# Graph attention kernel: in the spread stage one compare scalar per tile and three sums per edge lane instead of one

## The chip, the cores and the metric

The kernel runs on one core of a Trainium2 chip. The time is device microseconds of one execution; three runs of the kernel before gave 6165.33, 6170.83 and 6172.71 us. The core has five engines with queues of their own: PE (matrix products), DVE (vector work), ACT (activation functions, copies), POOL (GpSimd, here also the issuer of scattered writes) and SP (issues DMAs). They meet through semaphores only.

## The reference

A graph of 6250 nodes with 64 features and 206,250 edges (source, destination, 64 edge features), sorted by destination. First a graph attention layer with four heads, then two graph convolutions, each followed by a layer norm.

```python
out_i = act(jnp.concatenate([x_i, edge_attr], -1) @ W).reshape(-1, HEADS, DIM)   # act = softplus
out_j = act(jnp.concatenate([x_j, edge_attr], -1) @ W).reshape(-1, HEADS, DIM)
alpha = act((jnp.concatenate([out_i, out_j], -1) * att).sum(-1))
...                                    # norm over all edges, softplus, softmax over the edges of i
msg = out_j * alpha[:, :, None]
aggr = jax.ops.segment_sum(msg, i, num_segments=N_NODES)
...
msgs = h[src] * norm[:, None]          # graph convolution, twice
out = jax.ops.segment_sum(msgs, dst, num_segments=n)
```

## The kernel before, in words

`i` of the attention layer is the source, `j` the destination. Edges come sorted by destination, but the attention layer sums over sources. So the kernel puts them in another order in DRAM, and the stages follow one another, with a barrier between.

**Key stage** (`key_stage`). From the lists of sources and destinations it makes the counts and, for every edge, a pair of numbers in DRAM: minus the source's lane (its number modulo 128) and a code. The code is the source's block (number / 128) times 8, plus the destination modulo 8, plus 1024 times the destination's bin, which is the destination / 8. It also finds where each of the 784 bins begins in the sorted list (`startS`), and sets a flag when the data do not suit the fast path (then other, general stages run).

**Spread stage** (`spread_stage`, lines 710 to 1180). 202 steps of 1024 edges, 128 partitions by K = 8. In each step:
- PE, ACT: the destination's half of the layer, `out_j`, 256 numbers an edge (`product` L1120, `softplus` L1033, written into the tile `rowS`).
- DVE: `rank` (L927) finds the row of each edge in the new order. `dots` (L973) multiplies the 64 numbers of one head with their attention weights and sums them, for head 0 alone (DOTS = 1), in two parts of four lanes each.
- POOL: eight scattered writes a step (L889), each of 128 rows of RW = 323 numbers: 256 of `out_j`, 64 edge features, minus the source's lane, the destination, and the sum of head 0. A part is sent when its sums are made.
- In the first 196 steps, four bins a step: the counts matrix of the graph (`adj`), which the convolutions use. For each bin `load_pairs` (L835) on SP's queue fetches the pairs of the 384 edges that begin at the bin's start. `column` (L955) on DVE makes for each of three groups of 128 edges two one-hot tiles: `one_c` (L962), 392 columns of blocks by destination modulo 8, and `one_s` (L964), 128 lanes. L962 adds the bin's own number from `codes` to the column's number and compares the sum with the pair's code, so edges that belong to a later bin fall out. PE multiplies the two (L1144), ACT copies the counts (L1030), and after four steps, a block of 128 destinations, ACT stores 1568 KB (L1070).

What sets the order: each engine's queue is written out by hand. DVE's step is: rank, with two of the three columns of bin 1 put between its dependent instructions; the third column; bin 2; the one-hots of the next step's ranks and window (`hots`, `windows`); bin 3; part 0 of the sums; bin 0 of the next step; part 1 of the sums. On SP's queue, in the first 100 steps, two fills of 323 KB follow each block. Four `rowS` buffers let POOL be up to that many steps behind.

**Half stage** (`half_stage`). It reads the rows back in the new order, 912 tiles of 256 rows, in groups of BU = 6 with a buffer each. A buffer is loaded again (L1592) when the sums of its tile are made (`sp_read`). DVE makes one of the tile's two one-hots three tiles ahead (`places`, L1624), POOL the other (L1604), and POOL copies the edge features (L1612) and the lanes and ready sums (L1606). PE transposes them (`turn`), one tile ahead of the products (`product`, L1721 and L1726); its queue is in order, so the products of a tile wait for the transposes of the next. Then ACT (L1682, L1686), then DVE (`finish`, L1627): for each of 2 × 4 heads one sum. For head 0 only the source's half is still to sum, 64 numbers (L1638), and the ready part is added later (L1659); for heads 1 to 3 both halves, 128 numbers (L1643).

Later stages read the first 256 numbers of the rows; the softmax, message, node and convolution stages are not touched.

Of the kernel before, what the change touches and what calls it, by code (L numbers as in the profile page):

```python
# [15 lines left out]
fp32 = mybir.dt.float32  # L16
# [6 lines left out]
P = 128  # L23
# [15 lines left out]
DOTS = 1  # L39
DOT = C + D + 2  # L40
RW = DOT + DOTS
NR_BUF = 4
GQ = GB // NR_BUF
CODE = 1024
EXACT = 256
# [8 lines left out]
class Sizes:  # L54


    def __init__(self, nodes, edges):
# [20 lines left out]
        assert self.GC < CODE and self.GC <= 1024  # L78
# [80 lines left out]
def gnn_kernel(nc, x, src, dst, ea, W, att, bias, gamma, beta, W1, b1, W2, b2, out):  # L159
# [11 lines left out]
    def sb(ctx, name, shape, dt, side=None):  # L171
        return ctx.enter_context(nc.sbuf_tensor(own(name), shape, dt, side=side))
# [16 lines left out]
    with top:  # L189
# [33 lines left out]
        with ExitStack() as lists:  # L223
            m["ioc"] = sb(lists, "ioc", [P, z.GC], fp16)
# [45 lines left out]
def key_stage(nc, z, m, sb, ps, sem, x, src, dst):  # L270

    NB, HB, NG, T = z.NB, z.HB, z.NG, z.NG * K
    with ExitStack() as ctx:
# [12 lines left out]
        flatl = sb(ctx, "flatl", [P, T], i32)  # L286
# [30 lines left out]
        none = sb(ctx, "none", [P, GT, 2], fp32)  # L317
        psq = [ps(ctx, f"psq{n}", [P, 512], fp32) for n in range(2)]
# [90 lines left out]
        def _(eng):  # L409
# [14 lines left out]
            eng.iota(m["ioc"][:, :], [[1, z.GC]], base=0, channel_multiplier=0,  # L424
# [7 lines left out]
            eng.memset(blank[:, :, C + D:C + D + 1], 1.0).then_inc(blanked, 1)  # L432
# [15 lines left out]
        def _(eng):  # L448
# [21 lines left out]
            eng.tensor_scalar(flatl[:, :], flat[:, 0:T], EXACT - 1, None, ALU.bitwise_and).then_inc(v, c.up() and 1)  # L470
            eng.tensor_scalar(eighth[:, :], flat[:, 0:T], 3, None, ALU.arith_shift_right).then_inc(v, c.up() and 1)
            eng.wait_ge(v, c.n)
            eng.tensor_copy(flatb[:, :], flatl[:, :]).then_inc(low_ready, 1)
# [23 lines left out]
            eng.wait_ge(loaded, 16 * loads)  # L497
            eng.tensor_scalar(tmp[:, :, :], key[:, :, :], 7, None, ALU.arith_shift_right).then_inc(v, c.up() and 1)
# [11 lines left out]
            for n in range(2):  # L510
# [3 lines left out]
            eng.scalar_tensor_tensor(m["ends"][:, :, 0], tmp[:, 0, :], -1.0, neg[:, 0, :], ALU.mult,  # L514
                                     ALU.subtract).then_inc(v, c.up() and 1)
            eng.tensor_copy(m["ends"][:, :, 1].bitcast(i32), m["dst"][:, :]).then_inc(v, c.up() and 1)
# [7 lines left out]
            eng.scalar_tensor_tensor(neg[:, 1, :], tmp[:, 0, :], float(CODE), tmp[:, 1, :], ALU.mult,  # L524
                                     ALU.add).then_inc(v, c.up() and 1)
# [30 lines left out]
            eng.tensor_tensor(m["bad"][0:1, :], m["bad"][0:1, :], full8[:, :], ALU.add).then_inc(v, c.up() and 1)  # L556

# [152 lines left out]
def spread_stage(nc, z, m, sb, ps, sem, ea, att):  # L710
# [4 lines left out]
    with ExitStack() as ctx:  # L715
# [191 lines left out]
        def _(eng):  # L907
# [47 lines left out]
            def column(b, s, q, k):  # L955
                t = step(b, s)
                r = q % 2
                if k == 0:
                    eng.wait_ge(pair_in[q], (t + 1) * 16)
                    o, c = before(t, q, 2, GQ)  # L960
                    wait(eng, built[o], c)
                eng.tensor_scalar(one_c[r][:, k, :], m["ioc"][:, :], m["codes"][:, span(t * GQ + q, 1)],  # L962
                                  pair[q][:, k, 1:2], ALU.add, ALU.is_equal)
                ins = eng.tensor_scalar(one_s[r][:, k, :], m["io128b"][:, :], pair[q][:, k, 0:1], 0.0, ALU.add,  # L964
                                        ALU.is_equal)
                if k == GT - 1:
                    ins.then_inc(cols_made[q], 1)

            def adj(b, s, q):
                for k in range(GT):  # L970
                    column(b, s, q, k)
# [435 lines left out]
def table_stage(nc, z, m, sb, ps, sem, W):  # L1407
# [5 lines left out]
    with ExitStack() as ctx:  # L1413
# [47 lines left out]
        def _(eng):  # L1461
# [3 lines left out]
            eng.memset(fill[:, :, C + D:C + D + 1], 1.0).then_inc(zeroed, 1)  # L1465
# [1611 lines left out]
```

## Time and profile before

| | us |
|---|---|
| timed runs, median (lowest, highest) | 6170.83 (6165.33, 6172.71) |
| profiled execution, span | 6164.4 |
| DVE busy in the span | 4909.2 (80%) |
| PE busy | 4650.4 (75%) |
| ACT busy | 3996.8 (65%) |
| POOL busy | 3765.3 (61%) |
| spread stage, DVE / POOL busy in 290 to 2455 us | 1880 / 1648 |

The profile is of one execution, which the profiler times by its span. A row of a stretch gives each engine's busy time in it; a row of waits says who stood idle until what came; a row of the order of time gives start and duration in us, and in brackets the idle time before it and what ended that. Durations of neighbours on one engine overlap a little, so the distance from start to start is what an instruction costs. Issuing, register and semaphore instructions do not count as busy.

### The profile page before, as it was taken

To read this page: it belongs to the slowest core of one execution; us is meant where nothing else is said; L and a number is where in the kernel's file an instruction comes from. 1 tells how busy PE (TensorE), PEld (TensorE's weight loads), DVE (VectorE), ACT (ScalarE), POOL (GpSimd) and SP (SyncE) were. 2 spreads that over 40 slices of the span, in tenths; PEclk is the share of its full clock that TensorE was granted. 3 is DMA by queue.
4 is the path that set the end of the run, shared out by engine and by line. 5 is a ranking of instruction groups with operands and counts; after the bars stand their busy time and mean duration, and the time that the engine had idled before them with its cause. 6 is when DMAs were issued, how large, how long until landed. Compare 5 with 4: busy or idle time off the path is not lost. (4 is left out here: it accounts for less than half of the span.)

```text
span 6164.4 us, 164058 instructions
## 1 busy us (share of the span) xinstructions
PE 4650.4 (75%) x32887; PEld 3049.3 (49%) x32888; DVE 4909.2 (80%) x27493; ACT 3996.8 (65%) x10575; POOL 3765.3 (61%) x5381
## 2 busy tenths in 40 slices
PE   1377777777777774788888888888658888885799
PEld 0144444444444443445544544444335555554799
DVE  6588888989988984799999999999867777667233
ACT  3266666667666664688888888888767777776000
POOL 2277777777777777566666656565457777775000
PEclk8599999999999997899999999999879999997899
DMA  8867777776666665655555555555447777774898
GB/s 215 243 219 237 233 228 237 225 237 225 218 221 225 216 221 176 197 156 157 156 157 156 159 155 155 155 155 154 112 138 217 219 218 217 216 216 134 315 360 339
DMA packets 913878, 1262.07 MB, mean 205 GB/s; under 512 B 268468, under 2 KB 775459, under 8 KB 894916
## 3 DMA queue, kind: packets, MB, share of 16 engines
q1 hardware_dynamic: 785592, 859.76, 48.3%
q0 software_dynamic: 88560, 318.29, 14.0%
q10 hardware_dynamic: 39580, 82.35, 3.8%
q8 instruction: 57, 0.93, 0.1%
q14 instruction: 89, 0.73, 0.0%
HBM read 833.17 MB, written 426.91 MB: 204 GB/s over the span
## 5 line engine op out<-in xcount | busy, mean ns | idle before, releaser
L889 POOL DMA_INDIRECT rows<-rowS,idx x1616 | 1647.8, 1020 | 530.6 <-issue 505.7
L1643 DVE CUSTOM_DVE_ANT_1 junk<-bufh,attb 128x128 bf16<-128x128 f32 x5472 | 1369.1, 297 | 0.0
L1604 POOL TENSOR_SCALAR one<-io128b,bufh 128x128 bf16<-128x128 bf16 x912 | 752.8, 825 | 802.6 <-DMA bufh<-rows 802.6
L962 DVE TENSOR_SCALAR one_c<-ioc,codes,pairS 128x392 bf16<-128x392 f16 x2352 | 916.3, 390 | 214.3 <-DMA pairS<-pairs 205.5
L2369 PE MATMUL psm<-msg,onem 128*128 128x260 f32 x3648 | 916.1, 395 | 208.6 <-issue 168.9
L1144 PE MATMUL psa<-one_c,one_s 128*128 128x392 bf16 x2352 | 550.2, 345 | 546.2 <-ACT cnts L1030 297.7
L2290 POOL TENSOR_TENSOR msg<-oj,heads 128x512 f32<-128x512 f32 x760 | 799.8, 1075 | 209.7 <-DMA oj<-rows 176.9
L2369 PEld LDWEIGHTS psm<-msg,onem 128*128 128x128 f32 x3648 | 649.5, 190 | 474.8 <-issue 399.4
L1726 PE MATMUL pre<-P3h,oneT 128*128 x5472 | 756.4, 274 | 0.0
L1682 ACT ACTIVATE lg<-pre 128x512 f32<-128x512 f32 x912 | 545.0, 598 | 297.4 <-PE pre L1726 272.8
L2302 ACT ACTIVATE dist_m<-io,sums_lanes 128x128 f32<-128x128 f32 x1368 | 499.2, 396 | 293.4 <-PE psm L2369 262.6
L964 DVE TENSOR_SCALAR one_s<-io128b,pairS 128x128 bf16<-128x128 bf16 x2352 | 651.4, 277 | 0.0
L1037 ACT ACTIVATE lgS<-preS 128x1024 f32<-128x1024 f32 x404 | 413.2, 1023 | 359.1 <-PE preS L1133 355.1
L1721 PE MATMUL pre<-W2d,eaTh 64*128 64x256 f32 x3648 | 641.7, 429 | 0.0
L1726 PEld LDWEIGHTS pre<-P3h,oneT 128*128 128x128 bf16 x5472 | 460.5, 98 | 344.9 <-issue 302.8
L1686 ACT ACTIVATE bufh<-lg 128x512 f32<-128x512 f32 x912 | 576.5, 632 | 29.0
L1144 PEld LDWEIGHTS psa<-one_c,one_s 128*128 128x128 bf16 x2352 | 195.5, 100 | 720.9 <-DVE one_s L964 519.4
L1030 ACT ACTIVATE cnts<-psa 128x392 bf16<-128x392 f32 x784 | 363.3, 489 | 259.6 <-PE psa L1144 253.7
L1127 PE MATMUL preS<-W2d,eaT 64*128 64x256 f32 x3232 | 514.1, 441 | 6.6 <-ACT eaT L1048 6.6
L1638 DVE CUSTOM_DVE_ANT_0 junk<-bufh,attb 128x64 bf16<-128x64 f32 x1824 | 423.9, 232 | 74.0 <-ACT bufh L1686 70.1
L1710 PE MATMUL turned<-identb,one 128*128 128x128 bf16 x1824 | 255.0, 221 | 300.1 <-DVE one L1624 133.2
L2344 DVE TENSOR_TENSOR acc<-acc,psm 128x260 f32 x912 | 381.6, 418 | 113.2 <-DVE acc L2344 74.6
(299 smaller groups left out, 9020.0 us busy)
## 6 DMA issues: line engine op xcount, KB each, us to landing
bufh<-rows SPq DMA_DIRECT2D x912, 323.0 KB, 3.2
oj<-rows SPq DMA_DIRECT2D x912, 256.0 KB
adj<-adj SPq DMA_DIRECT2D x70, 1568.0 KB, 10.0
adj<-cnts ACTq DMA_DIRECT2D x49, 1568.0 KB
eaS<-in_edge_attr_dram SPq DMA_DIRECT2D x201, 256.0 KB
low<-dlow SPq DMA_DIRECT2D x202, 252.0 KB
adj_early<-adj SPq DMA_DIRECT2D x28, 1568.0 KB, 8.9
rows<-blanktail POOLq DMA_DIRECT2D x20, 1615.0 KB, 43.5
```

The source lines that it names most:

```text
L889: eng.indirect_dma_start(out=m["rows"][h], out_offset=bass.IndirectOffsetOnAxis(ap=idx[s][:, k:k + 1], axis=0), in_=rows[s][:, k, :], in_o ...
L962: eng.tensor_scalar(one_c[r][:, k, :], m["ioc"][:, :], m["codes"][:, span(t * GQ + q, 1)], pair[q][:, k, 1:2], ALU.add, ALU.is_equal)
L964: ins = eng.tensor_scalar(one_s[r][:, k, :], m["io128b"][:, :], pair[q][:, k, 0:1], 0.0, ALU.add, ALU.is_equal)
L1144: mm = eng.matmul(psa[r][:, 0:z.GC], one_s[r][:, k, :], one_c[r][:, k, :], start=(k == 0), stop=(k == GT - 1))
L1604: eng.tensor_scalar(one[j % PRE][:, 1, :], m["io128b"][:, :], buf[j][:, 1, 0, C + D:C + D + 1], 0.0, ALU.add, ALU.is_equal).then_inc(secon ...
L1643: ins = eng.tensor_tensor_reduce(junk[q][:, k * H + h, :, :], buf[j][:, k, :, h * D:(h + 1) * D], attb[:, :, h, :], 1.0, 0.0, ALU.mult, AL ...
L1682: eng.activation(lg[q][:, :, :], pre[q][:, :, 0:C], ACT.Exp, accum_out=m["exps"][:, span(2 * z.NG + i * BU + j, 1)]).then_inc(exp_done[j], 1)
L1686: eng.activation(buf[j][:, :, 1, 0:C], lg[q][:, :, :], ACT.Ln, bias=1.0).then_inc(sp_ready[j], 1)
L1721: eng.matmul(pre[j % PRE][:, k, 0:C], eaT[q][k * D:(k + 1) * D, :], m["W2d"][k * D:(k + 1) * D, :], start=True, stop=False, skip_group_che ...
L1726: mm = eng.matmul(pre[j % PRE][:, k, 0:C], oneT[q][:, k * P:(k + 1) * P], P3[:, bass.ds(b, 1), n, :].rearrange("p o c -> p (o c)"), start= ...
L2290: eng.tensor_tensor(msg[j][:, :, 0:C].rearrange("p k (h d) -> p k h d", h=H), oj[j][:, :, :, :], heads[:, :, j * UT:(j + 1) * UT].rearrang ...
L2369: mm = eng.matmul(psm[j][:, 0:C + H], one[q][:, k, :], msg[q][:, k, :], start=(k == 0), stop=(k == UT - 1))
```

## The change

The code of a pair now holds the destination's bin modulo four, times 512, instead of the bin times 1024. The table of column numbers `ioc` has four rows, one for each bin of a step, with 0, 512, 1024 and 1536 added. So L962's addition of `codes` goes, and the compare has one scalar from memory, the pair's code. `one_s` is compared with the lane itself, no longer with a sum against zero. The order of a bin's six compares is now three `one_c`, then three `one_s`, and the rank has the three `one_c` of bin 1 in its first gap and the three `one_s` in its second. Since a bin is told only modulo four, the key stage tests that bins four apart start at least 384 edges apart, and adds to the flag where they do not.

DOTS is 3: the spread stage sums heads 0, 1 and 2, and the half stage sums only the source's half for these, and both halves for head 3. The row has 325 numbers; destination and lane change places, so that lane and sums lie together.

```diff
-DOTS = 1
+DOTS = 3
 DOT = C + D + 2
+LANE = C + D + 1
...
+TURN = 512
...
-            m["ioc"] = sb(lists, "ioc", [P, z.GC], fp16)
+            m["ioc"] = sb(lists, "ioc", [P, GQ, z.GC], fp16)
...
-            eng.iota(m["ioc"][:, :], [[1, z.GC]], base=0, channel_multiplier=0,
+            eng.iota(m["ioc"][:, :, :], [[TURN, GQ], [1, z.GC]], base=0, channel_multiplier=0,
...
-            eng.tensor_copy(pair[:, :, 0], m["ends"][:, :, 0]).then_inc(v, c.up() and 1)
-            eng.tensor_scalar(tmp[:, 0, :], key[:, 1, :], 3, None, ALU.arith_shift_right).then_inc(v, c.up() and 1)
+            eng.tensor_scalar(pair[:, :, 0], m["ends"][:, :, 1], -1.0, None, ALU.mult).then_inc(v, c.up() and 1)
+            eng.tensor_scalar(tmp[:, 0, :], key[:, 1, :], (GQ - 1) * GD, None, ALU.bitwise_and).then_inc(v, c.up() and 1)
...
+            far = z.NR - GQ
+            eng.tensor_scalar(ended[:, 0:far], startf[:, GQ:z.NR], float(z.E), float(GT * P), ALU.is_ge,
+                              ALU.mult).then_inc(v, c.up() and 1)
+            eng.tensor_tensor(near8[:, 0:far], startf[:, GQ:z.NR], startf[:, 0:far],
+                              ALU.subtract).then_inc(v, c.up() and 1)
+            eng.wait_ge(v, c.n)
+            eng.tensor_tensor(near8[:, 0:far], near8[:, 0:far], ended[:, 0:far], ALU.add).then_inc(v, c.up() and 1)
+            eng.wait_ge(v, c.n)
+            eng.tensor_reduce(close8[:, :], near8[:, 0:far], AX.X, ALU.min).then_inc(v, c.up() and 1)
+            eng.wait_ge(v, c.n)
+            eng.tensor_scalar(close8[:, :], close8[:, :], float(GT * P), None, ALU.is_lt).then_inc(v, c.up() and 1)
+            eng.wait_ge(v, c.n)
+            eng.tensor_tensor(m["bad"][0:1, :], m["bad"][0:1, :], close8[:, :], ALU.add).then_inc(v, c.up() and 1)
...
-            def column(b, s, q, k):
+            def columns(b, s, q):
+
                 t = step(b, s)
                 r = q % 2
-                if k == 0:
-                    eng.wait_ge(pair_in[q], (t + 1) * 16)
-                    o, c = before(t, q, 2, GQ)
-                    wait(eng, built[o], c)
-                eng.tensor_scalar(one_c[r][:, k, :], m["ioc"][:, :], m["codes"][:, span(t * GQ + q, 1)],
-                                  pair[q][:, k, 1:2], ALU.add, ALU.is_equal)
-                ins = eng.tensor_scalar(one_s[r][:, k, :], m["io128b"][:, :], pair[q][:, k, 0:1], 0.0, ALU.add,
-                                        ALU.is_equal)
-                if k == GT - 1:
-                    ins.then_inc(cols_made[q], 1)
+                eng.wait_ge(pair_in[q], (t + 1) * 16)
+                o, c = before(t, q, 2, GQ)
+                wait(eng, built[o], c)
+                for k in range(GT):
+                    eng.tensor_scalar(one_c[r][:, k, :], m["ioc"][:, q, :], pair[q][:, k, 1:2], None, ALU.is_equal)
+
+            def lanes(b, s, q):
+
+                r = q % 2
+                for k in range(GT):
+                    ins = eng.tensor_scalar(one_s[r][:, k, :], m["io128b"][:, :], pair[q][:, k, 0:1], None,
+                                            ALU.is_equal)
+                ins.then_inc(cols_made[q], 1)
...
                 def between(k):
                     if dense(b):
-                        column(b, s, 1, k)
+                        (columns, lanes)[k](b, s, 1)
 
                 rank(b, s, h, between)
                 if dense(b):
-                    column(b, s, 1, 2)
                     adj(b, s, 2)
...
                     eng.tensor_copy(m["sums"][:, 0:1 + DOTS, span((i * BU + j) * UT, UT)],
-                                    buf[j][:, :, 0, C + D:DOT + 1:2].rearrange("p k n -> p n k"))\
+                                    buf[j][:, :, 0, LANE:DOT + DOTS].rearrange("p k n -> p n k"))\
```

On DVE, at the start of a step of the spread stage, the order before was this (`ranks` and `base` belong to the rank, `one_c` and `one_s` to a bin):

```order
L942 TENSOR_TENSOR ranks<-psr,base 128x400
L962 TENSOR_SCALAR one_c<-ioc,codes,pairS 128x392
L964 TENSOR_SCALAR one_s<-io128b,pairS 128x128
L948 TENSOR_TENSOR base<-base,psr 128x50
L950 TENSOR_TENSOR ranks<-ranks,ohr 128x400
L962 TENSOR_SCALAR one_c<-ioc,codes,pairS 128x392
L964 TENSOR_SCALAR one_s<-io128b,pairS 128x128
L953 TENSOR_REDUCE idx<-ranks 128x8
L962 TENSOR_SCALAR one_c<-ioc,codes,pairS 128x392
L964 TENSOR_SCALAR one_s<-io128b,pairS 128x128
```

In the changed kernel the same place reads:

```order
L960 TENSOR_TENSOR ranks<-psr,base 128x400
L981 TENSOR_SCALAR one_c<-ioc,pairS 128x392 x3
L966 TENSOR_TENSOR base<-base,psr 128x50
L968 TENSOR_TENSOR ranks<-ranks,ohr 128x400
L987 TENSOR_SCALAR one_s<-io128b,pairS 128x128 x3
L971 TENSOR_REDUCE idx<-ranks 128x8
L981 TENSOR_SCALAR one_c<-ioc,pairS 128x392 x3
L987 TENSOR_SCALAR one_s<-io128b,pairS 128x128 x3
```

Bin 1 is now finished before the reduction that makes `idx`, and each group of three compares of one kind stands together. After bin 3, and again after bin 0 of the next step, 12 sums follow where there were 4.

In the half stage DVE's sums for one of a tile's two columns of rows were these (the row with 128x1 reads the sum out of the accumulator):

```order
L1638 ISA junk,sums<-bufh,attb 128x64
L1638 ISA sums 128x1
L1643 ISA junk,sums<-bufh,attb 128x128
L1643 ISA sums 128x1
L1643 ISA junk,sums<-bufh,attb 128x128
L1643 ISA sums 128x1
L1643 ISA junk,sums<-bufh,attb 128x128
L1643 ISA sums 128x1
```

And in the changed kernel:

```order
L1659 ISA junk,sums<-bufh,attb 128x64
L1659 ISA sums 128x1
L1659 ISA junk,sums<-bufh,attb 128x64
L1659 ISA sums 128x1
L1659 ISA junk,sums<-bufh,attb 128x64
L1659 ISA sums 128x1
L1664 ISA junk,sums<-bufh,attb 128x128
L1664 ISA sums 128x1
```

The number of instructions is the same; two of the four sums are of half the length.

## Rows read from the trace of the kernel before

**Rows 1.** The page, its first line.

```profile
span 6164.4 us, 164058 instructions
```

**Rows 2.** Busy us (and count) by stretch, then PE clock, DMA share, GB/s.

```profile
core 0: us, PE busy (x) PEld busy (x) DVE busy (x) ACT busy (x) POOL busy (x), PEclk, DMA share, GB/s
...
290.00:2455.00 2165.00, 1564.62 (x12214) 980.32 (x12214) 1880.23 (x9397) 1404.25 (x2398) 1647.78 (x1616) 0.93 0.69 223
...
2600.00:4200.00 1600.00, 1377.92 (x9796) 797.63 (x9796) 1493.80 (x13070) 1322.87 (x3770) 965.45 (x2261) 1.00 0.56 156
```

**Rows 3.** Half stage, 2600 to 4200 us: loads of row tiles, and one wait.

```profile
bufh<-rows SPq DMA_DIRECT2D x754, 323.0 KB, 3.2
...
DVE junk L1638 <- ACT bufh L1686: 55.5, 111, 0.9
```

**Rows 4.** Waits, 290 to 2455 us: total us, times, longest.

```profile
POOL rows L889 <- issue: 505.7, 1570, 24.8
...
DVE one_c L962 <- DMA pairS<-pairs: 205.5, 49, 7.2
```

**Rows 5.** Order of time, DVE, spread stage: start, duration, engine, line.

```profile
1012.79 0.23 DVE L940 COPY rowS<-ends 128x16 f32 x1
...
1022.29 0.23 DVE L940 COPY rowS<-ends 128x16 f32 x1
...
1027.30 0.48 DVE L924 TENSOR_SCALAR ohT<-low,wsc 126x1024 bf16<-126x1024 bf16 x1
1027.69 0.37 DVE L962 TENSOR_SCALAR one_c<-ioc,codes,pairS 128x392 bf16<-128x392 f16 x1
1027.99 0.24 DVE L964 TENSOR_SCALAR one_s<-io128b,pairS 128x128 bf16<-128x128 bf16 x1
1028.15 0.37 DVE L962 TENSOR_SCALAR one_c<-ioc,codes,pairS 128x392 bf16<-128x392 f16 x1
...
1029.34 0.22 DVE L979 CUSTOM_DVE_ANT_0 weighed<-rowS,att_row 128x64 bf16<-128x64 f32 x1
1029.49 0.22 DVE L979 CUSTOM_DVE_ANT_0 weighed<-rowS,att_row 128x64 bf16<-128x64 f32 x1
1034.58 0.38 DVE L962 TENSOR_SCALAR one_c<-ioc,codes,pairS 128x392 bf16<-128x392 f16 x1 [4.86 <-DMA pairS<-pairs]
```

**Rows 6.** Order of time: the spread stage's last sum and last scatter.

```profile
2419.94 0.22 DVE L979 CUSTOM_DVE_ANT_0 weighed<-rowS,att_row 128x64 bf16<-128x64 f32 x1
...
2452.61 0.96 POOL L889 DMA_INDIRECT rows<-rowS,idx  x1 [0.30 <-issue]
```

**Rows 7.** Order of time, half stage: one loop from sums to sums.

```profile
3097.53 0.28 DVE L1643 CUSTOM_DVE_ANT_1 junk<-bufh,attb 128x128 bf16<-128x128 f32 x1
3097.74 0.27 DVE L1624 TENSOR_SCALAR one<-io128b,bufh 128x128 bf16<-128x128 bf16 x1
...
3101.51 0.76 POOL L1604 TENSOR_SCALAR one<-io128b,bufh 128x128 bf16<-128x128 bf16 x1 [1.19 <-DMA bufh<-rows]
...
3103.09 0.70 PE L1721 MATMUL pre<-W2d,eaTh 64*128 64x256 f32 x4
...
3106.07 0.29 DVE L1638 CUSTOM_DVE_ANT_0 junk<-bufh,attb 128x64 bf16<-128x64 f32 x1 [0.46 <-ACT bufh L1686]
```

**Rows 8.** One line each: durations and starts, or mean ns after the bar.

```profile
L962 DVE TENSOR_SCALAR one_c<-ioc,codes,pairS x2352: 362/373/586, 290.3 to 2360.8; 128x392 bf16<-128x392 f16 x196
...
L889 POOL DMA_INDIRECT rows<-rowS,idx x1616 | 1647.8, 1020 | 530.6 <-issue 505.7
...
L889 POOL DMA_INDIRECT rows<-rowS,idx x1616: 956/962/1431, 300.0 to 2452.6; - x180
...
L559 DVE TENSOR_SCALAR_CACHE_REDUCE hit<-hi_src 128x800 bf16<-128x800 bf16 x50 | 49.3, 986 | 1.7
```

**Rows 9.** Order of time: issues on SP's and ACT's queues.

```profile
1022.28 1.55 SPq L1403 DMA_DIRECT2D rows<-fill  x2
...
1022.71 0.34 ACTq L1070 DMA_DIRECT2D adj<-cnts  x1
```

More of the change, by code:

```diff
@@ L77, in __init__ @@
         self.NR = self.NB * GB
-        assert self.GC < CODE and self.GC <= 1024
+        assert self.GC + GD <= TURN and GQ * TURN <= 2048
 class Count:
@@ L317, in key_stage @@
         none = sb(ctx, "none", [P, GT, 2], fp32)
+        near8, ended = (step[0:1, :] for step in steps8)
+        close8 = sb(ctx, "close8", [1, 1], fp32)
         psq = [ps(ctx, f"psq{n}", [P, 512], fp32) for n in range(2)]
@@ L469, in _ @@
             eng.wait_ge(flat_in, 64)
-            eng.tensor_scalar(flatl[:, :], flat[:, 0:T], EXACT - 1, None, ALU.bitwise_and).then_inc(v, c.up() and 1)
+            eng.tensor_scalar(flatl, flat[:, 0:T], EXACT - 1, None, ALU.bitwise_and).then_inc(v, c.up() and 1)
             eng.tensor_scalar(eighth[:, :], flat[:, 0:T], 3, None, ALU.arith_shift_right).then_inc(v, c.up() and 1)
             eng.wait_ge(v, c.n)
-            eng.tensor_copy(flatb[:, :], flatl[:, :]).then_inc(low_ready, 1)
+            eng.tensor_copy(flatb[:, :], flatl).then_inc(low_ready, 1)
             eng.tensor_copy(base8[:, :], eighth[:, 0:1]).then_inc(v, c.up() and 1)
@@ L523, in _ @@
             eng.wait_ge(v, c.n)
-            eng.scalar_tensor_tensor(neg[:, 1, :], tmp[:, 0, :], float(CODE), tmp[:, 1, :], ALU.mult,
-                                     ALU.add).then_inc(v, c.up() and 1)
+            eng.scalar_tensor_tensor(neg[:, 1, :], tmp[:, 0, :], float(TURN // GD), tmp[:, 1, :],
+                                     ALU.mult, ALU.add).then_inc(v, c.up() and 1)
             eng.wait_ge(v, c.n)
@@ L953, in rank @@
                     eng.tensor_reduce(idx[s][:, :], ranks[:, :, :], AX.X, ALU.add).then_inc(idx_ready, 1)
-            def column(b, s, q, k):
+            def columns(b, s, q):
                 t = step(b, s)
                 r = q % 2
-                if k == 0:
-                    eng.wait_ge(pair_in[q], (t + 1) * 16)
-                    o, c = before(t, q, 2, GQ)
-                    wait(eng, built[o], c)
-                eng.tensor_scalar(one_c[r][:, k, :], m["ioc"][:, :], m["codes"][:, span(t * GQ + q, 1)],
-                                  pair[q][:, k, 1:2], ALU.add, ALU.is_equal)
-                ins = eng.tensor_scalar(one_s[r][:, k, :], m["io128b"][:, :], pair[q][:, k, 0:1], 0.0, ALU.add,
-                                        ALU.is_equal)
-                if k == GT - 1:
-                    ins.then_inc(cols_made[q], 1)
+                eng.wait_ge(pair_in[q], (t + 1) * 16)
[9 more added lines that the diff above has]
+                ins.then_inc(cols_made[q], 1)
             def adj(b, s, q):
-                for k in range(GT):
-                    column(b, s, q, k)
+                columns(b, s, q)
+                lanes(b, s, q)
             def dots(b, s, part):
@@ L1623, in places @@
                 wait(eng, o_turned[o], c)
-                eng.tensor_scalar(one[q][:, 0, :], m["io128b"][:, :], buf[j][:, 0, 0, C + D:C + D + 1], 0.0,
+                eng.tensor_scalar(one[q][:, 0, :], m["io128b"][:, :], buf[j][:, 0, 0, LANE:LANE + 1], 0.0,
                                   ALU.add, ALU.is_equal).then_inc(one_ready[j], 1)
@@ L1842, in places @@
                 wait(eng, o_turned[o], c)
-                eng.tensor_scalar(one[q][:, 0, :], m["io128b"][:, :], buf[j][:, 0, 2 * D:2 * D + 1], 0.0,
+                eng.tensor_scalar(one[q][:, 0, :], m["io128b"][:, :], buf[j][:, 0, 2 * D + 1:2 * D + 2], 0.0,
                                   ALU.add, ALU.is_equal).then_inc(one_ready[j], 1)
-                eng.tensor_copy(m["nloA"][:, span((i * BU + j) * UT, UT)], buf[j][:, :, 2 * D]).then_inc(lo_kept[j], 1)
+                eng.tensor_copy(m["nloA"][:, span((i * BU + j) * UT, UT)], buf[j][:, :, 2 * D + 1]).then_inc(lo_kept[j], 1)
             def finish(i, j):
```

17 lines of the change are left out of this document (9 added, 8 removed).

## The prediction

> **What bounds the kernel now.** I read the page first, then the busy time by stretch, then in each of the two touched stages the waits, and last the order of time inside one period of each.
>
> The span is 6164.4 us [rows 1]; the three timed runs have a median of 6170.8, so some 6 us lie around the span, and my sum is made on the span and given with those 6 added. Two stages carry the change. The spread stage runs from 290 to 2455 us, the half stage from about 2494 to about 4430: there 754 rows tiles are loaded in 1600 us [rows 2, 3], 2.12 us a tile, and it has 912 tiles.
>
> In the spread stage DVE is busy 1880 of 2165 us and POOL 1648 [rows 2], yet POOL is the bound. The reader is to see three things. POOL's idle time is 505.7 us in 1570 pieces put down to "issue" [rows 4], 0.3 us between one scatter and the next, so with a scatter of 0.96 us its least period is 1.26 us and 8 scatters a step cost at least 10.1 us. DVE, in a step without a wait, needs 9.50 us (from one copy of the ends at 1012.79 to the next at 1022.29 [rows 5]). And at the end DVE makes its last sum at 2419.94 and POOL starts its last scatter at 2452.61 [rows 6]: POOL is three steps behind. But DVE is nearly as full: it also waits 205.5 us for the pair lists, 49 times [rows 4], once for each of the 49 blocks. 196 × 9.5 + 205 = 2067 us against POOL's 2036 plus what collisions add. So DVE has no cover to give away: what DVE is given here beyond some 30 us is on the path.
>
> In the half stage DVE is busy 1494 of 1600 us and PE 1378 [rows 2], and TensorE's granted clock is 1.00, its upper level of 2.4 GHz. DVE looks like the bound, with 8 sums a tile. But it is not alone. Follow one loop [rows 7]. DVE ends the sums of a tile at 3097.74 (there the next tile's one-hot starts), which frees the tile's buffer; the next rows land and POOL starts its one-hot on them at 3101.51, 3.77 us later; POOL also copies the edge features, and only then does PE transpose them and start the product of the tile before, at 3103.09, 1.58 us later; PE, two ACT passes, and DVE starts the sums of that tile at 3106.07, 2.98 us later, having waited 0.46 us for ACT. These 8.33 us contain no sum at all. They span five tiles, and DVE waits at their end once in each group of six (111 waits, 55.5 us in the stretch [rows 3]).
>
> **What the change does, and what it costs.**
>
> Spread stage, sums. 202 steps × 8 lanes × 2 more heads = 3232 more sums on DVE. Two of them start 0.15 us apart (1029.34 and 1029.49, with the accumulator read between [rows 5]). 16 × 0.15 = 2.40 us a step; in the 196 steps that have bins, 470 us. Nothing hides them: DVE goes from one instruction to the next without a gap.
>
> Spread stage, one scalar in place of two in one_c. The trace has no fp16 tile compared with one scalar. The one_s instruction (128 elements, one scalar from memory) takes 0.16 us to the next start, ohT (1024 elements, one scalar) 0.39, one_c (392, two scalars) 0.30 [rows 5]. A line through the first two is 0.127 + 0.257 ns an element, so 392 elements with one scalar would take 0.23: 0.06 to 0.07 less than now. Taken: 0.065 × 2352 [rows 8] = 153 us. Below, it can be 0 (the second scalar is free and one_c is slow for its type); above, one_c cannot be cheaper than one_s with a third of its elements, so at most 0.14 × 2352 = 329. The row it is nearest to is the line's. one_s keeps one scalar in memory and loses only a constant: 0.
>
> The Trainium skill (VectorE: DVE Perf Modes, the section on the TRN2 errata) gives SBUF work on DVE as 58 cycles plus the elements over the mode's speed, with no term for the scalars. That rule speaks against this change: it would have one_c cost the same with one scalar as with two, and the 153 us would be 0. The rows do not bear it out, since one_c lies 0.07 us over the line of its neighbours; but they do not separate the second scalar from the other type, so it stays a rival, below.
>
> Spread stage, the wait for pairs. At the start of a block the queue of SP has two fills of 323 KB (first half only) at 1022.28 and ACT's store of 1568 KB goes out at 1022.71 [rows 9]; DVE comes for its pair list at 1029.6 and gets it at 1034.58, 4.86 us late [rows 5]: about 12 us from the store to the landing. With the longer step DVE comes later after that store: 1.6 us by the rest of the step in which the store goes out, 0.6 by its own next step up to that point, and perhaps 1 because the three compares of a tile now stand together ahead of the reduction, so that PE, ACT and the store get on sooner. Some 3 us of a mean wait of 4.2 go: 49 × 3 = 150 us. Bounds: 0 and 205.
>
> The end of the stage. The last compare starts at 2360.8 [rows 8]. 2361 + 470 − 153 − 150 = 2528. Then follow six steps without bins, in which POOL is the bound with 10.1 us each, 61 us, and about 5 us for its last part: 2594 against 2453.6. The stage grows by 140 us; POOL, now ahead of DVE, waits. With the bounds of the wait it is 85 to 290, with those of the scalar −35 to 295.
>
> POOL's scatters average 1020 ns and half of them take 962 or less [rows 8]; the rest is collisions with DVE. The Trainium skill (SBUF — State Buffer, "Who interferes with whom") says that DVE's two-port modes lock GpSimd out for the whole instruction. Shorter compares would by that cost POOL less than the 94 us they may cost now, but POOL no longer ends last, so the sum is the same.
>
> Half stage. Heads two and three come summed, so 4 of 8 sums a tile go from the 128-element form, 0.21 us (3097.53 to 3097.74 [rows 7]), to the 64-element form, 0.15: 0.26 us a tile at most counting 0.065 each. If DVE alone bound, 912 × 0.26 = 237 us. But the loop above has no sum in its 8.33 us. A group of six is now the first tile 1.88, the loop 8.33, the sums of the last tile 1.80 and 0.7 for the copies and the loop's branch, together 12.7, which is 6 × 2.12. After: 1.62 + 8.33 + 1.54 + 0.7 = 12.2. The four tiles in the middle save their 0.26 too, but wait for it at the loop's end. 152 groups × 0.52 = 79 us. Bounds: 237 above; below 40, if the denser loads lengthen the 3.77 us.
>
> The rest. The copies of sums (POOL's now 4 rows, DVE's addition now 3 heads) move one cost to another: 0. Rows are 1300 bytes, not 1292: 0.6% more bytes where the DMA share is 0.69 and 0.56 [rows 2]. The key stage gets six short instructions on one partition, of at most 784 elements; a row of 800 takes 0.99 us [rows 8]: +4 us. The longer iota is hidden by DVE's wait for the inputs.
>
> Sum: 6170.8 + 140 + 4 − 79 = 6236 us.
>
> **Rivals.**
>
> A, faster: the half stage gives all of its 237 us. It would if POOL's part of the loop shrinks as well, since POOL reads while DVE sums, or if buffers land sooner; then 6170.8 + 144 − 237 = 6078. It decides from about 0.16 us saved per tile on. For it: DVE is busy 93% there. Against it: the wait for ACT, once a group, is there already now. A milder form with the waits for pairs all gone and 150 us from the half stage gives 6110. Together 20%.
>
> B, no change: the same two in part, half stage 130 to 160 us: 6160 to 6180. 9%.
>
> C, the second scalar is free (the errata rule above): 153 us more, 6389; at half that price, 6310. 10%.
>
> D, the wait for pairs stays at 205 us since the store ends it and the store moves along with the step: 150 more, 6386. For it: the store follows the step's last tile. 10%.
>
> E, POOL stays the bound and hides the new sums: the stage stays at 2165 and the kernel takes about 6095. It needs a DVE step under 10.6 us; 9.50 + 2.40 − 0.78 = 11.1 before any wait. 3%, counted in A.
>
> F: the added test on near starts sets the flag and the general path runs, at least a second half stage, over 8000 us. Four bins hold about 1000 edges and the test asks for 384: 1%.
>
> **The numbers.** My forecast, 6236, has about 50%; its own range is 6190 to 6290. Taking in part of A below and of C and D above, 8 in 10 lie in 6120 to 6330. A change of under 0.2%, 12 us, can't be told from none. Faster by more: 20%; within: 9%; slower: 71%.
>
> **What would show it.** In the spread stage: one_c about 320 ns at the median in place of 373, dots 24 a step, a step of 11.1 us, POOL with real waits for DVE's sums, ACT's waits for sent rows gone, waits for pairs near 60 us. In the half stage: a tile of 2.03 us, DVE busy under 90%, and its wait for ACT grown to some 200 us or more. The forecast is wrong if a half-stage tile takes under 1.95 us, if one_c's duration does not fall, or if POOL is still never idle in the spread stage.

## The result, and the profile after

The changed kernel takes 6537.9 us (median of 4 runs, 6537.3 to 6545.8), the one before, on the same chip, 6168.7 (6165.3 to 6172.7): a ratio of 1.0594, 95% interval 1.0579 to 1.0609. The forecast was 6236, the range 6120 to 6330. The profiled execution's span grew from 6164.4 [rows 1] to 6544.1 us, by 380.

First the page after, of which three lines matter: the span and two of the DMA queues (packets, MB, share of 16 engines' time). The instruction queue q14 had 89 packets and 0.73 MB before.

```profile
span 6544.1 us, 169809 instructions
...
q14 instruction: 313, 2.56, 0.1%
q8 instruction: 57, 0.93, 0.1%
```

Then the stretches of the two stages, which answer to [rows 2]. The columns are the same.

```profile
290.00:2925.00 2635.00, 1697.20 (x12220) 1045.51 (x12218) 2189.03 (x15861) 1418.62 (x2399) 1589.66 (x1616) 0.84 0.56 184
3100.00:4700.00 1600.00, 1437.55 (x10309) 848.31 (x10309) 1397.08 (x13744) 1373.92 (x3968) 939.48 (x2380) 1.00 0.60 165
```

The spread stage is 470 us longer (2635 against 2165), and DVE is busy in it for only 309 us more. DVE was busy 87% of the stage before, 83% after: it has more to do and stands idle more. The half stage runs denser, as forecast. So the question is what DVE's new idle time is. These are the waits of the spread stage after (total us, times, longest), to be read against [rows 4]:

```profile
POOL rows L907 <- issue: 484.9, 1417, 26.6
POOL rows L907 <- DVE rowS L1001: 374.7, 71, 11.9
DVE rowS L958 <- issue: 341.6, 43, 10.9
...
DVE ohr L932 <- issue: 42.2, 22, 2.8
...
DVE one_c L981 <- DMA pairS<-pairs: 14.3, 6, 4.4
```

The wait for pairs went from 205.5 us to 14.3. In its place DVE stands 341.6 us ahead of L958 and 42.2 us ahead of L932, and "issue" says that nothing which the profile shows held it. POOL, which before waited 3.0 us for DVE's sums in all, now waits 374.7. The order of time on DVE shows where this lies, in a block of the first half of the destinations:

```profile
1209.62 0.21 DVE L1001 CUSTOM_DVE_ANT_0 weighed<-rowS,att_row 128x64 bf16<-128x64 f32 x1
...
1209.76 0.21 DVE L1001 CUSTOM_DVE_ANT_0 weighed<-rowS,att_row 128x64 bf16<-128x64 f32 x1
1209.90 0.08 DVE L1001 DVE_READ_ACCUMULATOR2_ANT rowS<- 128x1 f32 x1
1215.89 0.18 DVE L958 COPY rowS<-ends 128x16 f32 x1 [5.91 <-issue]
...
1218.76 0.78 DVE L981 TENSOR_SCALAR one_c<-ioc,pairS 128x392 bf16<-128x392 f16 x3
1219.45 0.57 DVE L987 TENSOR_SCALAR one_s<-io128b,pairS 128x128 bf16<-128x128 bf16 x3
1221.78 0.58 DVE L932 TENSOR_TENSOR ohr<-io,hi_src 128x400 bf16<-128x400 bf16 x1 [1.77 <-issue]
```

and in one of the second half:

```profile
2541.80 0.18 DVE L958 COPY rowS<-ends 128x16 f32 x1 [10.87 <-issue]
...
2545.85 0.57 DVE L932 TENSOR_TENSOR ohr<-io,hi_src 128x400 bf16<-128x400 bf16 x1
```

L958 is the first instruction of DVE's loop body, which holds one block of four steps. There are two such loops, one for each half of the destinations, of 23 and 22 passes; the first and the last block of a half stand outside as straight code. In the first loop there is a gap of some 6 us at the start of a pass and one of some 1.9 us a little later; in the second one of about 10 us and no second one. The 43 gaps ahead of L958 are 22 and 21: one each time that a loop returns to its start, none at its first pass.

### The profile page after: what moved, and what is told of

It reads as the page before. It is cut to its first block and busy times, and to the rows that moved or that the text cites. A ratio compares the mean times of both kernels' runs of the same rounds, so it can differ in the third digit from the quotient of the medians.

```text
span 6544.1 us, 169809 instructions
## 1 busy us (share of the span) xinstructions
PE 4771.8 (73%) x32887; PEld 3123.7 (48%) x32888; DVE 5020.0 (77%) x33963; ACT 3990.7 (61%) x10575; POOL 3621.3 (55%) x5381
## 5 line engine op out<-in xcount | busy, mean ns | idle before, releaser
L907 POOL DMA_INDIRECT rows<-rowS,idx x1616 | 1589.7, 984 | 1056.4 <-issue 484.9
L1165 PE MATMUL psa<-one_c,one_s 128*128 128x392 bf16 x2352 | 571.1, 357 | 889.2 <-DVE one_s L987 837.3
L1625 POOL TENSOR_SCALAR one<-io128b,bufh 128x128 bf16<-128x128 bf16 x912 | 715.7, 785 | 796.0 <-DMA bufh<-rows 795.7
L1659 DVE CUSTOM_DVE_ANT_0 junk<-bufh,attb 128x64 bf16<-128x64 f32 x5472 | 1018.0, 233 | 146.2 <-ACT bufh L1707 129.7
L1001 DVE CUSTOM_DVE_ANT_0 weighed<-rowS,att_row 128x64 bf16<-128x64 f32 x4848 | 743.2, 216 | 3.1 <-ACT rowS L1061 3.1
L981 DVE TENSOR_SCALAR one_c<-ioc,pairS 128x392 bf16<-128x392 f16 x2352 | 627.3, 319 | 23.4 <-DMA pairS<-pairs 14.3
L1148 PE MATMUL preS<-W2d,eaT 64*128 64x256 f32 x3232 | 571.4, 482 | 7.0 <-ACT eaT L1069 7.0
L1664 DVE CUSTOM_DVE_ANT_1 junk<-bufh,attb 128x128 bf16<-128x128 f32 x1824 | 534.7, 293 | 0.0
L987 DVE TENSOR_SCALAR one_s<-io128b,pairS 128x128 bf16<-128x128 bf16 x2352 | 457.7, 251 | 0.0
```

The costliest lines, as they stand in the source:

```text
L907: eng.indirect_dma_start(out=m["rows"][h], out_offset=bass.IndirectOffsetOnAxis(ap=idx[s][:, k:k + 1], axis=0), in_=rows[s][:, k, :], in_o ...
L981: eng.tensor_scalar(one_c[r][:, k, :], m["ioc"][:, q, :], pair[q][:, k, 1:2], None, ALU.is_equal)
L1001: ins = eng.tensor_tensor_reduce(weighed[:, k, n, :], rows[s][:, k, n * D:(n + 1) * D], att_row[:, n, :], 1.0, 0.0, ALU.mult, ALU.add, row ...
L1148: eng.matmul(pre[h][:, q, a * C:(a + 1) * C], eaT[j][q * D:(q + 1) * D, 2 * h + a, :], m["W2d"][q * D:(q + 1) * D, :], start=(a == 0), sto ...
L1165: mm = eng.matmul(psa[r][:, 0:z.GC], one_s[r][:, k, :], one_c[r][:, k, :], start=(k == 0), stop=(k == GT - 1))
L1625: eng.tensor_scalar(one[j % PRE][:, 1, :], m["io128b"][:, :], buf[j][:, 1, 0, LANE:LANE + 1], 0.0, ALU.add, ALU.is_equal).then_inc(second_ ...
```

## The experiments

Theory A, a guess that the experiments were to test: DVE's instruction memory holds four pieces of 128 instructions and loads one piece ahead of the one it is in. A loop that touches at most three pieces stays in it. One that touches four pushes out its own start, and each pass begins with a load of instructions from DRAM. I counted every instruction of DVE's list (waits, register operations and branches too). The loop body of the spread stage had 260 and has 372. The trace's records agree: 260 and 372 a pass, and in the changed kernel 1049 from the first loop's last return to the second's first. (The list has one jump to the very next instruction in between that the trace does not record, and it is not counted.) Where a piece begins was fitted to one observation: the small gap of the first half stands ahead of the loop's 27th instruction (L932), so the loop's first is at place 102 of a piece (counted from 0). Every other place follows by counting. B is the same with two pages of 256, C that the place of the code does not matter.

All ten kernels were timed in three rounds against the kernel before on their chips (there 6189 to 6194 us, 0.3 to 0.4% more than on the chip of the result, so that times of different rows are best compared by their ratios). "Last sum" is the start of the last L1001 of the spread stage, "half" the time from the half stage's first sum to its last, both in the profiled execution. Pieces are those that DVE's two loops of the spread stage touch. "Once" and "in 2" are single gaps outside the loops, behind the inserted increments; 1.6 us of the gaps of experiments 1 and 5 and the 0.7 and 0.6 us of 6 and 7 are of that kind too.

| kernel | pieces | gaps ahead of the loop, us | wait for pairs | last sum | half | ratio (95%) |
|---|---|---|---|---|---|---|
| before | 3, 3 | 0 | 205.5 | 2419.9 | 1931 | 1 |
| changed | 4, 4 | 341.6 + 42.2 | 14.3 | 2888.6 | 1835 | 1.0594 (1.0579 to 1.0609) |
| 1 changed, shifted 30 | 3, 4 | 121.9 | 88.3 | 2704.0 | 1839 | 1.0252 (1.0235 to 1.0269) |
| 2 changed, both loops shifted | 3, 3 | 10.7 in 2 | 98.2 | 2593.6 | 1842 | 1.0091 (1.0074 to 1.0108) |
| 3 codes only | 3, 3 | none | 266.8 | 2374.7 | 1937 | 0.9898 (0.9881 to 0.9914) |
| 4 two heads | 3, 4 | 196.5 | 99.5 | 2565.1 | 1888 | 1.0128 (1.0111 to 1.0145) |
| 5 before, shifted 32 | 4, 3 | 191.1 | 97.9 | 2535.2 | 1939 | 1.0147 (1.0130 to 1.0164) |
| 6 two heads, shifted | 3, 3 | 0.7 | 135.6 | 2411.8 | 1889 | 0.9877 (0.9861 to 0.9894) |
| 7 as 6, pairs early | 3, 3 | 0.6 | 1.8 | 2376.6 | 1891 | 0.9823 (0.9806 to 0.9840) |
| 8 as 3, pairs early | 3, 3 | none | 2.4 | 2363.3 | 1936 | 0.9871 (0.9855 to 0.9888) |
| 9 before, shifted 64 | 3, 3 | 4.5, once | 218.9 | 2439.5 | 1936 | 0.9996 (0.9987 to 1.0006) |
| 10 as 2, pairs early | 3, 3 | 10.7 in 2 | 2.0 | 2496.3 | 1839 | 0.9933 (0.9916 to 0.9949) |

**1. The changed kernel, shifted.** Thirty increments of a semaphore that nobody waits for, ahead of DVE's first loop:

```diff
+        padded = sem(ctx, "padded")
             eng.wait_ge(att_row_in, 16)
+            for _ in range(30):
+                eng.sem_inc(padded, 1)
             by_half(eng, blocks)
```

> The changed kernel with 30 semaphore increments more on DVE's queue ahead of its first loop of the spread stage; nothing else differs, and they cost about 1 us. Three theories of the gaps at the start of DVE's loop (341.6 us before L958, 42.2 us before L932 in the changed kernel). Theory A: the loop's 372 instructions are fetched again on each pass because they touch four pieces of 128 instructions (a piece is one 8 KB packet of the instruction queue), and only a loop that touches three stays. The 30 instructions move the first loop (destinations of the first half) onto three pieces, the second loop stays on four: the gaps of about 6 + 1.6 us a pass go in the first loop (some 170 us), those of 10.4 us stay in the second; as the waits for pairS come back in part (about 2 us a block, 50 us), the time is about 6400 us. Theory B: the same with two pages of 256 instructions: both loops then fit, no gap is left, 6200 to 6250 us. Theory C: the gap has nothing to do with where the code lies (a full DMA queue, a late semaphore at the start of a block): nothing changes, 6538 us.

It took 6351.6 us against 6192.9. The waits of DVE, first in 290 to 1450 us, then in 1450 to 2740:

```profile
DVE one_c L982 <- DMA pairS<-pairs: 84.3, 25, 6.5
...
DVE rowS L959 <- issue: 1.6, 1, 1.6
```

```profile
DVE rowS L959 <- issue: 120.4, 21, 6.9
...
DVE one_c L982 <- DMA pairS<-pairs: 4.0, 3, 3.1
```

The first loop lost its gaps, the second kept one at each return: A and neither B nor C. The instruction queue says the same more directly. From 450 to 1300 us, inside the first loop, the queue moves no packet at all; from 1600 to 2600 us, some 20 passes of the second, it moves

```profile
q14 instruction: 101, 0.83, 0.3%
```

which is five a pass: the four pieces of the loop and one ahead. In the changed kernel the first of these stretches has 81 packets, in the kernel before none. The second loop now begins at place 29, so that 99 of its instructions lie in the first piece, and its gap fell from 10 to 5.7 us, which I had not expected (I had left it at 10.4, hence 6400 for the time). This fits the two patterns of the changed kernel: where few instructions stand ahead of the next piece (1 in the second half, 26 in the first), the pass seems to wait for that piece too. No run tests this reading by itself.

**2. Both loops shifted.** 30 increments ahead of the first loop and 104 between the two, so that they begin at places 4 and 5.

> The changed kernel with 30 semaphore increments ahead of DVE's first loop of the spread stage and 104 more between its two loops (some 5 us). Theory A (pieces of 128 instructions): both loops of 372 instructions now touch three pieces; all gaps go, 384 us less, and about 50 to 100 us of waits for pairS come back: 6210 to 6280 us, where the prediction (6236 us) had put the change itself. The instruction queue's packets fall from 313 to about 90. Theory B: with two pages of 256 the first loop fits and the second too: as A. Theory C (address doesn't matter): 6538 us plus 5.

6248.9 us, inside what was expected, with 98 packets on q14, and neither loop has a gap. DVE's waits from 290 to 2630 us:

```profile
DVE one_c L982 <- DMA pairS<-pairs: 98.2, 42, 6.1
DVE rowS L959 <- issue: 10.7, 2, 9.1
```

The two gaps left (1.6 us at 293.6 and 9.1 at 1483.2) stand in straight code right behind the 30 and the 104 increments, which take about 0.1 us each and do not count as busy: they are the price of the shift. 134 instructions without any work, on the engine that sets the stage, take the ratio from 1.0594 to 1.0091. This is the change as the prediction had priced it, 0.9% slower.

```profile
290.00:2630.00 2340.00, 1653.93 (x12218) 1022.06 (x12216) 2192.47 (x15861) 1419.21 (x2398) 1611.33 (x1616) 0.90 0.65 207
```

DVE is busy 2192 us as in the changed kernel (2189), in 295 us less of time.

**3 and 4. The codes alone (DOTS = 1), and two heads (DOTS = 2)**, each a change of one line: `DOTS = 3`.

> The changed kernel with DOTS = 1: the codes modulo four with one scalar, but only head 0 is summed in the spread stage, as before. The loop has 244 instructions and touches three pieces: no gaps. Half stage as before. If DVE's step sets the block: 2352 one_c less by 0.065 us each, 153 us, so 6020 us if the waits for pairS do not grow. Rival: each block ends no sooner because the loads of pairS (205.5 us of waits before) are held by what lies ahead of them on SP's queue, so that the waits grow by what one_c loses: 6150 to 6170 us. Taken value 6090 us.

> The changed kernel with DOTS = 2: heads 0 and 1 summed in the spread stage. DVE's loop has 308 instructions; by its place the first loop touches three pieces of 128, the second four. Theory A: no gaps in the first loop, gaps of about 10 us a pass in the second (22 passes, 220 us). Sum from before: +1616 sums of 0.15 = +242, one_c -153, gaps +220, waits for pairS -110 (they go in the second loop), half stage -48: about 6320 us. Theory B (two pages of 256): the second loop, from place 127 or 255 of a page, is cut as well only if a page begins right behind its start: the same. Theory C (gaps come with DVE's work in a step or with the queue's load): about equal gaps in both loops or none in either.

The codes alone: 6127.6 us, 1% faster than before, where 6090 was taken, between 6020 and a rival of 6150 to 6170: neither holds whole. DVE's busy time fell by 138 us (1880 to 1742), the wait for pairs rose from 205.5 to 266.8, and the last sum came only 45 us earlier. POOL's row of the whole stage shows why (busy, mean ns of one, then idle time):

```profile
L907 POOL DMA_INDIRECT rows<-rowS,idx x1616 | 1606.1, 994 | 525.7 <-issue 486.6 <-PE preS L1154 21.1 <-DVE rowS L1001 12.2
```

POOL fills 1606 + 526 = 2132 us, the whole stage, and waits 12 us for DVE. It sets the pace here, as in the kernel before. Its scatters became shorter, 994 ns for 1020 [rows 8], 42 us in all. The trace of the kernel before is from a chip on which it runs 0.3 to 0.4% faster; against experiment 9, from a chip like this one, the last sum comes 65 us earlier, 41 of them in the scatters and 24 in POOL's idle time. All kernels with the short compares have scatters of 984 to 1000 ns, the three with the long ones 1014 to 1020. The Trainium skill (SBUF — State Buffer, "Who interferes with whom") says that DVE in a two-port mode and GpSimd shut each other out for a whole instruction, whoever comes first; shorter compares and shorter scatters agree with it, but no run here held the rest equal.

Two heads: 6273.0 us where about 6320 was expected. In the first loop DVE has no gap; in the second it has 196.5 us of them:

```profile
DVE rowS L958 <- issue: 196.5, 21, 9.9
```

The loop has 308 instructions: at place 38 it touches three pieces, at place 127 four. Theory A told this from the count alone, before the run; B would have told the same, so this run speaks against C only.

**5 and 9. The kernel before, shifted.** The edit of experiment 1 in the old kernel, with 32 and with 64 increments; nothing of the change is in it.

> The kernel before, untouched but for 32 semaphore increments (about 1 us) on DVE's queue ahead of its first loop of the spread stage. Its loops have 260 instructions and touch three pieces of 128. The 32 move the first one so that its first instruction is the last of a piece and it touches four; the second loop, as all later ones, stays on three. Theory A (pieces of 128, a loop that touches four is fetched again on each pass): gaps of about 10 us before L940 in some 23 passes of the first loop and none in the second. A block of four steps is now 42.8 us long, set by POOL; DVE's work in it is 38.4, so that a gap of 10 us makes it some 6 us longer: 23 x 6 = 140 us more than before (100 to 170), a ratio of 1.02. Theory B (two pages of 256): the loop lies in two pages as before: no change. Theory C (the gap came with the work that the change added): no change.

> Control to the kernel before with 32 increments: the same with 64, so that both loops touch three pieces of 128 again (their first instructions at places 31 and 72 of a piece). Theory A: no gap ahead of L940 and the time of the kernel before within 0.3% (the increments cost some 2 us). Rival (the increments themselves, or any shift, disturb the loop): 1 to 3% slower, as with 32.

With 32, one loop of 260 instructions begins at place 127 and touches four pieces: 1.5% slower, by 91 us, where 140 was expected and 100 to 170 allowed: a miss in size, in part because its 22 gaps are of 8.6 us and not of 10. With 64 the time is that of the kernel before. With 32, the page's instruction queue and DVE's waits from 290 to 1450 us read:

```profile
q14 instruction: 200, 1.64, 0.1%
```

```profile
DVE rowS L941 <- issue: 191.1, 23, 9.2
...
DVE one_c L963 <- DMA pairS<-pairs: 16.0, 3, 7.3
```

and with 64, the waits from 290 to 2480 us:

```profile
q14 instruction: 91, 0.75, 0.0%
```

```profile
DVE one_c L963 <- DMA pairS<-pairs: 218.9, 49, 7.5
...
DVE rowS L941 <- issue: 4.5, 1, 4.5
```

The kernel is the same but for the increments, so the gap belongs neither to the new sums nor to a changed load of the DMA queues, and with 64 increments there is none, so it does not belong to the increments.

**6 and 7. A version that beats both.** Experiment 6 is two heads with 10 and 12 increments (places 48 and 21). Experiment 7 adds eight buffers for the pairs in place of four, loaded a step earlier:

```diff
-                wait(eng, cols_made[q], t)
+                wait(eng, cols_made[q], t - 1)
+                q += s % 2 * GQ
...
-                more = dense(near[0])
+                more = exists(*two) and dense(two[0])
                 if more:
-                    load_pairs(*near, 0)
+                    load_pairs(*two, 0)
```

> Two heads in the spread stage (DOTS = 2), with 10 and 12 semaphore increments ahead of DVE's two loops of the spread stage, so that both touch three pieces. Theory A: the 196.5 us of gaps of the unshifted kernel with DOTS = 2 go, about 50 to 90 us of waits for pairS come back: 110 to 150 us less than it, 1.2% under the kernel before. Rival: the gaps only turn into waits for pairS: as the unshifted one, 1.3% over the kernel before.

> As the aligned kernel with two heads, and the pairs of a step are loaded one step earlier, into eight buffers instead of four. If the waits for pairS (about 150 us expected there) come from the time that a load takes to land behind the fills and the store of counts, they go. DVE's work in the spread stage is then some 10.0 us a step against POOL's 10.5, so that POOL sets the stage, which ends where that of the kernel with the codes alone does: 50 us less than without the early loads, 2% under the kernel before. Rival: the waits come from SP's queue being held by other waits ahead of the loads, which an earlier place in the order does not help: no change.

6118.9 and 6086.3 us: 1.2% and 1.8% under the kernel before (0.9877 and 0.9823). Without the gaps the waits for pairs grew by 36 us, where 50 to 90 was expected; the early loads gave 33 us and not 50. In the second, the waits of 290 to 2500 us:

```profile
POOL rows L911 <- issue: 493.6, 1537, 25.2
...
DVE rowS L962 <- DMA rows<-rowS,idx: 68.8, 47, 5.1
...
POOL rows L911 <- DVE rowS L1007: 7.0, 23, 0.3
```

POOL waits for next to nothing, DVE waits for POOL's buffers: POOL is the bound. The last sum is at 2376.6 us, where the codes alone have it at 2374.7. So the second head costs 13 us in the spread stage (against experiment 8, below, at 2363.3) and gives 45 in the half stage.

**8 and 10. What the waits for pairs are worth.** The early loads with the codes alone, and with three heads and both loops shifted.

> The codes alone (DOTS = 1) with the pairs loaded one step earlier. In the kernel with the codes alone DVE waited 266.8 us for pairS, but POOL stood 525.7 us of which 486.6 were its own issue and only 12.2 a wait for DVE. If POOL sets that stage, the waits for pairS were slack: they go, DVE waits for free rowS buffers in their place, and the time stays within 0.2%. Rival: the waits for pairS set the stage: up to 200 us less.

> The changed kernel with three heads, both loops moved onto three pieces (30 and 104 increments) and the pairs loaded one step earlier. With three heads DVE sets the spread stage, so that here the waits for pairS (98.2 us in the aligned kernel) are time: 80 to 100 us less than the aligned kernel, 6150 to 6165 us where the kernel before takes 6193, a ratio of 0.994. It stays above the kernel with two heads and early pairs (0.9823), since DVE's step is then 0.9 us longer than POOL's and the half stage gives back only 45 us more. Rival: POOL or the waits for rowS set the stage even so: no gain over the aligned kernel (1.009).

With the codes alone 264 of 267 us of waits go and the ratio falls by 0.0027, some 17 us (0.9871 against 0.9898, the intervals overlap): they were slack but for that, and 188.8 us of waits for free `rowS` buffers stand in their place (waits of 290 to 2500 us).

```profile
DVE rowS L961 <- DMA rows<-rowS,idx: 188.8, 67, 5.9
...
DVE one_c L985 <- DMA pairS<-pairs: 2.4, 1, 2.4
```

With three heads 96 of 98 us of waits go and the ratio falls by 0.0158, 98 us (6147.4 us and 0.9933 for 6248.9 and 1.0091): there DVE is the bound and a wait of DVE is time. The same wait was worth next to nothing in one kernel and all of its length in the other.

## Why the prediction was wrong

The step that failed is the one on the sums of the spread stage: "Nothing hides them: DVE goes from one instruction to the next without a gap." The 3232 sums were priced by the time that each takes on DVE. They are two instructions each, 128 more in a body that had 260 (372, since the codes save 16 register operations), and the place that they take in instruction memory had no term, no bound and no rival. It cost 384 us of gaps. Between the changed kernel and experiment 2 the ratio falls by 0.050, 310 us, and the last sum comes 295 us sooner: the 384 us, less 84 of waits for pairs that had been hidden behind them (14.3 to 98.2), less the 10.7 of the increments, are 289. The other 15 us of the ratio were not traced. Rivals C and D, which pointed the same way, are both refuted. The trace of before could not show the gap, but two rows were there to ask about: the instruction queue's 89 packets, and a loop branch that cost DVE nothing, both true only as long as the loops fit.

The rest, by the prediction's own terms:

- **The scalar.** 0.065 us for each one_c was taken. The median fell from 373 ns [rows 8] to 309, the mean from 390 to 319. In the order of time above three of them take 0.69 us to the next start, 0.23 each as the prediction's line had it; over the middle of the stage the median from start to start falls from 0.287 to 0.231, by 0.056. Right, and some 20 us high. The edit took away the second scalar and the addition with it; one_s lost an addition of a constant and stayed at 0.162, which points at the scalar in memory; the new order of the compares was not tried apart. The Trainium skill's formula behind rival C (VectorE: DVE Perf Modes, the section on the TRN2 errata), which has no term for scalars, would leave one_c unchanged: the measurement decides.

```profile
L981 DVE TENSOR_SCALAR one_c<-ioc,pairS x2352: 300/309/510, 290.9 to 2844.0; 128x392 bf16<-128x392 f16 x196
```

- **The sums.** In the order of time above two sums start 0.14 us apart (0.146 is the median), 0.15 was the price. A step of DVE should be 11.1 us; in experiment 10, where DVE waits for next to nothing, the last sum at 2496.3 and a start near 290 make it 10.9 for 202 steps. Right.
- **The wait for pairs.** 150 of 205 us should go and 55 stay. Without gaps (experiment 2) 98.2 stay. Right in kind, 43 us short in size; with the gaps nearly all went.
- **The stage without gaps** should be 140 us longer. Against the kernel before as shifted in experiment 9, on chips where the kernel before takes 6189 and 6193 us, the last sum moved from 2439.5 to 2593.6, by 154, of which some 6 are the added increments. Right.
- **The half stage.** 79 us less was taken, with 237 if DVE alone bound. 912 tiles took 1931 us and take 1835 (from the first and last starts below, before and after): 96 less. Each head moves 47 us (1937, 1888, 1842 with one, two, three heads), 0.05 us of the 0.13 us a tile that its two shorter sums save. Right in kind and 17 us low. That the loop through POOL, PE and ACT is what holds the rest was not tested by itself. The sign that I named is half there: DVE is busy 87%, but its wait for ACT grew from 55.5 us to 108.2 in 1600, and not to 200 or more.

```profile
L1638 DVE CUSTOM_DVE_ANT_0 junk<-bufh,attb x1824: 208/216/377, 2501.0 to 4431.6; 128x64 bf16<-128x64 f32 x183
L1643 DVE CUSTOM_DVE_ANT_1 junk<-bufh,attb x5472: 276/282/409, 2501.2 to 4432.2; 128x128 bf16<-128x128 f32 x196
```

```profile
L1659 DVE CUSTOM_DVE_ANT_0 junk<-bufh,attb x5472: 207/217/381, 2968.6 to 4803.7; 128x64 bf16<-128x64 f32 x196
L1664 DVE CUSTOM_DVE_ANT_1 junk<-bufh,attb x1824: 275/281/372, 2969.0 to 4803.9; 128x128 bf16<-128x128 f32 x183
```

```profile
DVE junk L1659 <- ACT bufh L1707: 108.2, 201, 1.1
```

- **POOL as the bound before** (8 scatters of 1.26 us a step) was right, and experiments 3 and 8 bear it out. I did not draw the consequence: with the shorter compares and early pairs one more head (1.2 us a step) fits under POOL's step almost whole, and two do not.
- **The other rivals.** A and B needed 130 us and more from the half stage, which gives 96. E, POOL hiding the new sums, nearly holds for one more head (13 us, experiment 7) and not for two. The flag did not set (F). Without the gaps the change comes out at 1.0091 where 1.0106 was forecast. So near a hit is in part luck: the waits for pairs had been put 43 us too low and the half stage's saving 17 us too low, and they lean opposite ways.

## What to carry to other kernels

A rolled loop has a size, in instructions of each engine, and a place. Count the whole body (waits, register operations, accumulator reads) before more is unrolled into it, and when a loop's first instruction shows a gap that nothing explains, look at the packets of the instruction queue and shift the loop by some empty instructions: it is the cheapest test there is, and here the cure as well. And before waits of an engine are counted as time to be won, look whether the engine downstream has any idle time at all: 264 us of DVE's waits were worth some 17 us, 96 us of them were worth 98.

## What the runs showed of the hardware

The place of a loop decides. The same body of 372 instructions runs without a gap from place 4 or 5 of a piece of 128, and at each return has one of 5.7 us from place 29, two of 5.7 and 1.9 from 102, and one of 10.3 from 127. A body of 308 runs without from 38 and has 9.4 from 127; one of 260 runs without from 95, 8, 31, 72 and 40, and has 8.6 from 127. The 24 loops of the twelve kernels fit one rule: a gap at each return if the loop touches four pieces of 128, none if three. The fit hangs on the one count above: with the unrecorded jump counted, the loops at 127 would begin at 0, and the rule would give them no gap. The packets of the instruction queue, which need no count, agree: none in the middle of a loop that touches three pieces, five a pass in one that touches four. A packet is 8 KB (0.73 MB in 89). Why the gap from place 127 is 10.3, 9.4 and 8.6 us in bodies of 372, 308 and 260 stays open.

The Trainium skill (Runtime: NRT & Kernel Launch, "Instruction fetch mechanics") has it that most engines have room for 512 instructions and that a taken branch out of what is held forces a fetch: the runs agree, and give the price, 5.7 to 10.3 us a return for DVE in these loops, where the DMA engines are 52 to 65% busy. By its 32 KB for 512 instructions, as an estimate, a packet of 8 KB is 128 of them, the length of a piece. It also says that the room is two lines of 256. The runs differ: in two pages of 256, placed as the gaps of the changed kernel demand, the second loop of experiment 1 and the first of experiment 5 would have fitted, and both had gaps. The measurement decides. How the price depends on the load of the DMA queues was not tried.
